# Attention of a two-layer model: values times probabilities in three passes of split operands, two heads side by side

## The reference

```python
q = (hidden_states @ Wq.T).reshape(b, s, NH, HD).transpose(0, 2, 1, 3)
k = (hidden_states @ Wk.T).reshape(b, s, NKV, HD).transpose(0, 2, 1, 3)
v = (hidden_states @ Wv.T).reshape(b, s, NKV, HD).transpose(0, 2, 1, 3)
scores = jnp.einsum('bhqd,bhkd->bhqk', qf, kf)           # k and v repeated for 4 heads each
scores = jnp.where(causal, scores, neg)
attn = jax.nn.softmax(scores, axis=-1).astype(v.dtype)
out = jnp.einsum('bhqk,bhkd->bhqd', attn, v_rep)
out = out.transpose(0, 2, 1, 3).reshape(b, s, NH * HD)
return out @ Wo.T + bo
```

## Time and profile before

| | us |
|---|---|
| median of 3 runs | 1169.13 (1166.28 to 1170.8) |
| the profiled execution | 1162.17 |
| its span, first to last instruction | 1160.4 |
| TensorE busy in the span | 1098.4 (95%) |
| VectorE | 829.4 (71%) |
| ScalarE | 628.2 (54%) |
| GpSimd | 209.6 (18%) |

### The profile page before, as it was taken

The page is one execution under the profiler, slowest core; times in us unless marked ns, Lnnn a source line. Parts: engine busy times, 40 slices in busy tenths (PEclk is TensorE's granted clock), DMA queues, the critical chain, the costliest instruction groups (busy, mean ns, idle before and its releaser), DMA issues. The chain is left out here.

```text
span 1160.4 us, 26495 instructions
## 1 busy us (share of the span) xinstructions
PE 1098.4 (95%) x9990; PEld 937.1 (81%) x9990; DVE 829.4 (71%) x2423; ACT 628.2 (54%) x1607; POOL 209.6 (18%) x246
## 2 busy tenths in 40 slices
PE   6999999999999998999999999959889999998898
PEld 4898899889988998788888889846667777777687
DVE  5777467656765785867776775798998798877454
ACT  5644444444544453544434443457877877766552
POOL 0422222222222221441000000031022102220110
PEclk9999999999999999999999999978899999997899
DMA  9200000000000000201000000011000001100323
GB/s 310 89 6 2 1 1 1 1 1 1 1 1 1 1 1 22 80 1 29 1 1 1 1 1 1 32 60 32 3 34 33 25 10 34 33 2 2 103 69 105
DMA packets 26701, 32.90 MB, mean 28 GB/s; under 512 B 4960, under 2 KB 21968, under 8 KB 26576
## 3 DMA queue, kind: packets, MB, share of 16 engines
q1 hardware_dynamic: 26576, 31.22, 8.6%
HBM read 29.04 MB, written 2.17 MB: 27 GB/s over the span
## 5 line engine op out<-in xcount | busy, mean ns | idle before, releaser
L333 DVE TENSOR_TENSOR a_ps<-a_ps,causal 128x256 f32<-128x256 f32 x128 | 54.6, 427 | 92.8 <-PE a_ps L642 92.8
L1547 PE MATMUL b_ps<-ln_high,b_high 128*128 128x512 f32 x256 | 101.2, 395 | 1.1 <-ACT gate_up_raw L1462 1.1
L692 PE MATMUL a_ps<-a_wo_high,a_oT 128*128 128x256 f32 x512 | 101.2, 282 | 0.1
L1547 PE MATMUL b_ps<-ln_low,b_high 128*128 128x512 f32 x256 | 100.4, 392 | 0.0
L1547 PE MATMUL b_ps<-ln_high,b_low 128*128 128x512 f32 x256 | 100.1, 391 | 0.0
L316 POOL TENSOR_TENSOR a_probs<-a_probs,a_inv 128x256 f32<-128x256 f32 x64 | 40.1, 627 | 330.0 <-DVE a_inv L353 330.0
L1581 PE MATMUL b_ps<-b_wd_high,b_mid 128*128 128x256 f32 x512 | 96.4, 283 | 0.0
L508 ACT CAST a_oT<-a_ps 128x512 fp32r<-128x512 f32 x64 | 37.5, 586 | 107.2 <-PE a_ps L670 107.2
L494 ACT ACTIVATE a_probs<-a_ps,a_negmax 128x128 f32<-128x128 f32 x128 | 47.1, 368 | 89.2 <-DVE a_negmax L339 76.5
L1462 ACT ACTIVATE gate_up_raw<-b_ps 128x512 f32<-128x512 f32 x64 | 37.5, 598 | 95.7 <-PE b_ps L1547 95.6
L1347 DVE TENSOR_TENSOR gate_up_raw<-gate_up_raw,b_ps 128x512 f32<-128x512 f32 x64 | 42.9, 685 | 61.9 <-ACT gate_up_raw L1462 31.9
(11 more groups left out here) (434 smaller groups left out, 3010.0 us busy)
## 6 DMA issues: line engine op xcount, KB each, us to landing
gate_up_raw<-a_scratch SPq DMA_DIRECT2D x8, 768.0 KB, 3.7
gate_up_raw<-in_D_main SPq DMA_DIRECT2D x8, 304.5 KB
x<-in_hidden SPq DMA_DIRECT2D x4, 512.0 KB, 10.7
a_raw<-in_A_q SPq DMA_DIRECT2D x4, 512.0 KB, 7.6
gate_up_raw<-in_A_o SPq DMA_DIRECT2D x1, 2048.0 KB, 13.9
gate_up_raw<-in_B_g SPq DMA_DIRECT2D x1, 2048.0 KB, 12.3
gate_up_raw<-in_B_u SPq DMA_DIRECT2D x1, 2048.0 KB, 8.4
out<-x SPq DMA_DIRECT2D x8, 256.0 KB, 3.1
```

The lines of the kernel that those rows point to most:

```text
L333: nc.vector.tensor_tensor(diagonals, diagonals, r.causal[:].rearrange("p (o k) -> p o k", o=1).to_broadcast([P, 2, P]), ALU.add).then_inc( ...
L692: mm = nc.tensor.matmul(ps[:, out_bank(job), 0:HID], opart, wpart, start=(k == 0 and j == 0), stop=(k == QUARTER - 1 and j == len(passes) ...
L1547: mm = nc.tensor.matmul(ps[:, bank, :], wpart, xpart, start=(j == 0), stop=(j == len(passes) - 1))
```

## The change

- `values` works on a pair of heads and is called in the even steps (for heads `h - 2` and `h - 1`) and behind the last step. `v` and `pT` are kept as high and low parts, and each product becomes three passes with 512 and with 256 columns (two heads side by side).
- ScalarE rounds the turned probabilities (`round_pT`), ahead of the exponentials of the step; in step 15 also those of head 15, ahead of the next keys and queries. VectorE's copy becomes a subtraction. `take_v` on ScalarE gets a subtraction on VectorE behind it (`v_rest_of`), and only that frees the bank.
- The outputs of values of a pair lie in two banks, one for each sequence. `copy_oT` is called in the even steps and `split_oT` in the odd ones, with two instructions of 512 columns each.
- The high parts of `v` and the low part of `pT` live in the place of the gate weights. Of these only expert 2 is loaded where all eight were; the others are issued when the last values are done, and the experts' stage waits for them.

```diff
+FIRST_EXPERT, LATE_EXPERTS = (2, 3), ((3, 8), (0, 2))
...
+        PAIR = 2
+        pT_high = sb("pT_high", [P, GROUP_BATCHES, 3, PAIR, P], F32R)
+        pT_low = at("pT_low", [P, GROUP_BATCHES, 3, PAIR, P], next_weights.raw_at + LATE_EXPERTS[0][0] * EXPERT)
...
-                next_weights.load(sp, 0)
+                next_weights.load(sp, 0, *FIRST_EXPERT)
...
+                sp.wait_ge(next_weights.loaded[0], 16)
+                sp.wait_ge(oT_ready, GROUPS * NH // PAIR)
+                for experts_of in LATE_EXPERTS:
+                    next_weights.load(sp, 0, *experts_of)
...
                 def copy_pT(G):
                     for b in range(GROUP_BATCHES):
-                        dve.wait_ge(pT_ready, 2 * G + b + 1)
-                        if G >= 2:
-                            dve.wait_ge(oT_ready, G - 1)
-                        nc.vector.tensor_copy(pT[:, G % 2, b, :], ps[:, PTB[b], 0:QW]).then_inc(pT_copied, 1)
+                        dve.wait_ge(pT_rounded, 2 * G + b + 1)
+                        if G >= PAIR:
+                            dve.wait_ge(oT_ready, G // PAIR)
+                        nc.vector.tensor_tensor(pT_low[:, b, :, G % PAIR, :], turned_bank(b),
+                                                pT_high[:, b, :, G % PAIR, :].bitcast(F32), ALU.subtract
+                                                ).then_inc(pT_copied, 1)
+
+                def v_rest_of(i, t):
+                    dve.wait_ge(v_rounded, i * GROUP_TILES + t + 1)
+                    nc.vector.tensor_tensor(v_low[t], ps[:, PROJ[t % 2], :], v_high[t].bitcast(F32), ALU.subtract
+                                            ).then_inc(v_taken, 1)
...
-                def split_oT(G):
-
-                    dve.wait_ge(oT_copied, G + 1)
-                    nc.vector.tensor_tensor(oT[:, 1, G % RING, :], ps[:, OTB[G % 2], :],
-                                            oT[:, 0, G % RING, :].bitcast(F32), ALU.subtract).then_inc(oT_split, 1)
+                def split_oT(Q):
+
+                    for b in range(GROUP_BATCHES):
+                        dve.wait_ge(oT_copied, GROUP_BATCHES * Q + b + 1)
+                        nc.vector.tensor_tensor(out_rows(1, Q, b), out_bank_of(b), out_rows(0, Q, b).bitcast(F32),
+                                                ALU.subtract).then_inc(oT_split, 1)
...
-                    if G >= 2:
-                        split_oT(G - 2)
+                    if h % PAIR and G > PAIR:
+                        split_oT(G // PAIR - 1)
+                    if h == 0:
+                        for t in range(GROUP_TILES):
+                            v_rest_of(i, t)
...
+                def round_pT(G):
+                    for b in range(GROUP_BATCHES):
+                        act.wait_ge(pT_ready, 2 * G + b + 1)
+                        if G >= PAIR:
+                            act.wait_ge(oT_ready, G // PAIR)
+                        nc.scalar.copy(pT_high[:, b, :, G % PAIR, :], turned_bank(b)).then_inc(pT_rounded, 1)
...
+                    if h >= 1:
+                        round_pT(G - 1)
                     exps(G, 0)
                     exps(G, 1)
                     if h + 1 < NH:
                         take_q(G + 1)
-                    if G >= 1:
-                        copy_oT(G - 1)
+                    if h % PAIR == 0 and G >= PAIR:
+                        copy_oT(G // PAIR - 1)
...
+                    if h == NH - 1:
+                        round_pT(G)
                     if h == NH - 1 and i < LAST_GROUP:
                         take_k(i + 1, 0)
                         take_q(G + 1)
...
                     for b in range(GROUP_BATCHES):
-                        pe.wait_ge(pT_copied, 2 * G + b + 1)
...
+                        pe.wait_ge(pT_copied, 2 * (G + 1) + b + 1)
+                        turned = [x[:, b].rearrange("p s h q -> p (s h q)") for x in (pT_high, pT_low)]
+                        for t, cols, out in ((2 * b, slice(0, 4 * P), slice(0, 4 * P)),
+                                             (2 * b + 1, slice(4 * P, 6 * P), slice(2 * P, 4 * P))):
+                            passes = split_passes(v_high[t][:, g], v_low[t][:, g], turned[0][:, cols], turned[1][:, cols])
+                            for j, (vpart, ppart) in enumerate(passes):
+                                mm = nc.tensor.matmul(ps[:, OTB[b], out], vpart, ppart, start=(t == 2 * b and j == 0),
+                                                      stop=(t > 2 * b and j == len(passes) - 1))
...
-                    if h >= 1:
-                        values(i, h - 1)
-                    elif i >= 1:
-                        values(i - 1, NH - 1)
+                    if h and h % PAIR == 0:
+                        values(i, h - PAIR)
+                    elif h == 0 and i >= 1:
+                        values(i - 1, NH - PAIR)
...
-                values(LAST_GROUP, NH - 1)
+                values(LAST_GROUP, NH - PAIR)
```

More of the change, by code:

```diff
@@ L208, in attention, with at @@
         qT = later[:, NKV * GROUP:(NKV + 2) * GROUP].rearrange("p (s t) -> p s t", t=GROUP)
-        v_rest = later[:, (NKV + 2) * GROUP:(NKV + 4) * GROUP].rearrange("p (t n) -> p t n", n=NKV * HD)
-        v_first = ahead.xn[:].rearrange("p t d -> p (t d)").rearrange("p (t n) -> p t n", n=NKV * HD)
-        v = [half[:, t, :] for half in (v_first, v_rest) for t in range(GROUP_TILES // 2)]
+        EXPERT = DC * FE * WORD
+        def at(name, shape, offset):
+            return nc.alloc_sbuf_tensor_at("a_" + name, shape, F32R, offset=offset)
+        TWO_TILES = [P, GROUP_TILES // 2, NKV * HD]
+        v_highs = (at("v_high0", TWO_TILES, next_weights.raw_at + LATE_EXPERTS[-1][0] * EXPERT),
+                   at("v_high1", TWO_TILES, next_weights.raw_at + 6 * EXPERT))
+        v_lows = (at("v_low0", TWO_TILES, ahead.xn_at), at("v_low1", TWO_TILES, kept.xnT_at + (NKV + 2) * GROUP * WORD))
+        v_high, v_low = [[half[:, t, :] for half in halves for t in range(GROUP_TILES // 2)] for halves in (v_highs, v_lows)]
         negmax = sb("negmax", [P, 2, GROUP_TILES])
@@ L461, in _ @@
                         add_out(out_jobs(i, h)[1])
-                split_oT(head(LAST_GROUP, NH - 2))
-                split_oT(head(LAST_GROUP, NH - 1))
+                split_oT(GROUPS * NH // PAIR - 1)
                 for job in last_jobs:
@@ L478, in take_v @@
                     if i >= 1:
-                        act.wait_ge(oT_ready, head(i, 0))
-                    nc.scalar.copy(v[t], ps[:, PROJ[t % 2], :]).then_inc(v_taken, 1)
+                        act.wait_ge(oT_ready, head(i, 0) // PAIR)
+                    nc.scalar.copy(v_high[t], ps[:, PROJ[t % 2], :]).then_inc(v_rounded, 1)
+                def round_pT(G):
[4 more added lines that the diff above has]
+                        nc.scalar.copy(pT_high[:, b, :, G % PAIR, :], turned_bank(b)).then_inc(pT_rounded, 1)
                 def take_q(G):
@@ L499, in exps, with copy_oT @@
                                          accum_out=rowsum[:, s, 2 * b + 1:2 * b + 2]).then_inc(exp_ready, 1)
-                def copy_oT(G):
-                    act.wait_ge(oT_ready, G + 1)
-                    if G == 0:
+                def copy_oT(Q):
+                    act.wait_ge(oT_ready, Q + 1)
+                    if Q == 0:
                         act.wait_ge(w_split, len(BLOCKS_AT))
-                    if G >= RING:
-                        act.wait_ge(out_ready, ((G - RING) // QUARTER + 1) * GROUP_TILES)
-                    nc.scalar.copy(oT[:, 0, G % RING, :], ps[:, OTB[G % 2], :]).then_inc(oT_copied, 1)
+                    if PAIR * Q >= RING:
+                        act.wait_ge(out_ready, ((PAIR * Q - RING) // QUARTER + 1) * GROUP_TILES)
+                    for b in range(GROUP_BATCHES):
+                        nc.scalar.copy(out_rows(0, Q, b), out_bank_of(b)).then_inc(oT_copied, 1)
                 def weight_highs(k):
@@ L566, in _ @@
                         take_q(G + 1)
-                copy_oT(head(LAST_GROUP, NH - 1))
+                copy_oT(GROUPS * NH // PAIR - 1)
             @block.tensor
@@ L684, in project_out @@
                         pe.wait_ge(out_taken, job)
-                    pe.wait_ge(oT_split, (quarter + 1) * QUARTER)
+                    pe.wait_ge(oT_split, (quarter + 1) * QUARTER // PAIR * GROUP_BATCHES)
                     rows = slice(t * P, (t + 1) * P)
@@ L1084, in __init__, with load @@
         self.router_loaded = ctx.enter_context(nc.semaphore("router_loaded"))
-    def load(self, sp, k):
-        sp.dma_start(self.raw[:, k], self.sources[k].rearrange("e (c p) f -> p e c f", p=P)
+    def load(self, sp, k, first=0, end=NE):
+        sp.dma_start(self.raw[:, k, first:end], self.sources[k][first:end].rearrange("e (c p) f -> p e c f", p=P)
                      ).then_inc(self.loaded[k], 16)
@@ L1474, in _ @@
                     take_high(k, 0)
+                act.wait_ge(gate_up_weights.loaded[0], 16 * (1 + len(LATE_EXPERTS)))
```

34 lines of the change are left out of this document (21 added, 13 removed).

## The result

The changed kernel takes 1189.81 us (median of 4 runs, 1186.5 to 1199.05), the kernel before 1168.91 beside it (1166.28 to 1170.8): a ratio of 1.020, 95% interval 1.016 to 1.024. Slower by 21 us, as forecast in sign and inside the range of 1173 to 1194; 1183 was forecast, and 1190 lies above the 1178 to 1188 to which the prediction gave its 0.52. Its profiled execution took 1188.63 us (span 1186.7).

A forecast was written before the change was run, and what follows sets the result against it. TensorE, 99% busy, was taken as the bound, with new waits outweighing 17.2 us of saved work: +2.6 for group 0, +4.1 each for groups 1 and 2, group 3 +1.7 and +3.5, together +14: 1183 us, range 1173 to 1194.

The forecast's parts named there:

- The odd step: Steps 5, 7, 9, 11, 13, without values: 4.97 us against 6.07, the next scores released by ScalarE's query copy.
- the even one: Step after an odd one: 6.96 us (+0.89), with a pair's values at 2.08 and transposes 0.12 later for GpSimd.
- keys of steps 1 and 3: Groups 1 to 3: keys wait 1.5 us for VectorE's output job addition, now behind two oT subtractions.
- step 15 stops: At the group's end the next keys come 1.06 us later, TensorE stands 3.3 us; step 15 costs +2.44.
- the output job: In step 15, 2.04 us behind the transposes instead of 0.57, since ScalarE first rounds head 15 and copies keys.
- Rounding and subtracting: Each 384-column piece: 0.49 us for ScalarE's rounding, about 0.55 for VectorE's subtraction, the latter no change from the copy.
- the rival of dearer pieces: Each rounding or subtracting piece takes what 512 columns take (0.58, 0.66), odd steps 0.3 to 0.4 longer: 1190; chance 0.17.
- The clock: TensorE's granted clock stays at 1.00 in the attention, as at the 0.77 us stop; no time counted for a fall.
- its fall at the borders: Rival: 3.3 us stops of step 15 halve the clock, 1.2 us three times, +3.6; 1187 in all, chance 0.15.
- a sign of being wrong: Listed signs: a group of 106, rounding or subtracting beyond 0.6 us, or a clock under 1.00 within the attention.
- The first group's forecast of +2.6: Group 0, no output jobs before step 6: steps 1 and 3 gain 1.27 and 1.36, step 4 loses 1.83; +2.6.
- The last transposes: Group 3's step 15: the last transposes wait 0.49 us more for GpSimd, part of that step's +3.5.

The follow-up runs named there:

- Placement alone: Kernel before, plain fp32 values of two heads together in even steps, their oT copies there and subtractions in odd steps, no rounding or passes: 1185.22 us, ratio 1.0167.
- the two changed orders: Changed kernel, VectorE adding the output job before oT subtractions (steps 1, 3) and earlier in step 15, ScalarE copying keys and queries before rounding head 15: 1168.41 us.
- ScalarE's order alone: Changed kernel, only ScalarE's step 15 altered: next group's keys and queries copied ahead of rounding head 15; 1184.43 us, ratio 1.014 against the kernel before.
- each head by itself: Changed kernel's passes and rounding, but one head's values in every step, passes of 256 and 128 columns: 1178.66 us, ratio 1.009 against the kernel before.
- the values inside the odd steps: Changed kernel, a pair's passes right behind odd steps' scores, ahead of the turning, other engines' orders altered too: 1165.83 us; kernel before in the same order 1172.48.
- the last order: Run with passes inside odd steps, plus layer norm pieces behind the maxima, inversion earlier in steps 10 and 12, layer norm halves swapped: 1161.91 us, ratio 0.9966.

## Why the prediction was right, and which terms were off

**The mechanism held.** The odd step ends on ScalarE's query copy (4.84, forecast 4.97), GpSimd holds the transposes of the even one (7.04, forecast 6.96), values 2.12 (2.08), keys of steps 1 and 3 wait 1.4 us for the addition (1.5), step 15 stops 3.31 us (3.3), the output job starts 1.93 us behind the transposes instead of 0.57 (2.04). Placement alone and the two changed orders show the same from the other side: the waits come with the placement, and put in another order the queues give the 21 us back.

**Where the odd step was off.** 4.97 was forecast for 4.85. The prediction let three of the six transposes end 0.28 us ahead of the last; they are issued 0.109 apart, so it is 0.33, and ScalarE's rounding starts at 1.84, not 1.90. The rest is small change in ScalarE's pitches.

**Rounding and subtracting** at 0.49 and 0.55 were right (0.48 and 0.55 on the mean), so the rival of dearer pieces was wrong, though its 1190 is the nearest to the time measured.

**The clock was the mis-sized term.** The prediction put it at nothing, on the ground that a stop of 0.77 us had left it at 1.00, and gave 0.15 to its fall at the borders (1187). By its own list, a clock under 1.00 within the attention was a sign of being wrong, and that sign came. A stop of 0.77 says little about one of 3.3. The clock fell at all three borders, for 4.4 us where the rival had 3.6, and once where no rival had it, at the last group's wait of 3.62 us. There it cost 2.55: from those transposes to the experts' stage it is 16.35 us (468.60 to 484.95), and 13.80 (468.20 to 482.00) in the run with ScalarE's order alone, where the clock stayed at 1.00. Together 6.9 us. That 14 and 7 make the 21 by which the medians differ is in part luck: by the attention time the change costs 23.2.

The rule of the Trainium skill that the prediction weighed (TensorE: Matmul & The Clock Gate, HAM oscillation: a stream with waits between bursts can fall back to half rate in each round) agrees with the trace at the three borders; with the placement alone one border of three went without it.

**Smaller ones.** Between the two marks the forecast was +14.3 and 23.2 was measured; the clock leaves 2.0 us. Of these 0.9 is step 2 of the first group (7.89, forecast 7.01). In step 1 VectorE splits the output weights beside GpSimd's normalising, whose first piece takes 1.50 us instead of 0.61. It did so in the kernel before too, but after an odd step without values nothing hides it, and the transposes of step 2 wait:

```profile
31.94 1.50 POOL L344 TENSOR_TENSOR a_probs<-a_probs,a_inv 128x256 f32<-128x256 f32 x1 [7.91 <-DVE a_inv L388]
```
```profile
31.78 1.19 DVE L408 TENSOR_TENSOR a_wo_low<-gate_up_raw,a_wo_high 128x1024 fp32r<-128x1024 f32 x1
```
```profile
34.50 0.88 PE L702 MATMUL a_ps<-ident,a_probs 128*128 128x128 f32 x6 [0.74 <-POOL a_probs L346]
```

The rest is 0.1 to 0.2 us in each of steps 0 to 3, against steady pairs 0.05 shorter than forecast. The last transposes stood 7.45 us behind their scores, 6.96 before: the forecast 0.49. The first group's forecast of +2.6 does not follow from the terms that stand beside it, which give +2.2; 4.8 was measured, 1.56 of it the clock.

**What stays open.** Why one stop of 2.81 us left the clock alone and two others did not, why 3.60 us left it alone where 3.40, 3.62 and 3.95 brought it down, and why stops of 1.25 and 0.59 us were enough in the run with each head by itself; and why it stayed low to 238.7 in one run and to 241 in another. From the traces at hand such a term could be given only a chance. The 2 us by which the stages behind the attention were longer in the profiled execution (701.8 against 699.6) lie within what the same stages show in the other kernels (699.6 to 705.3) and are not put down to the change.

## What to carry to other kernels

Before work is taken from the bounding engine or moved on it, ask what hangs over the end of that work on the other engines: here 1.31 us at the end of every step hid three chains, and moving it (18.9 us with nothing else changed) cost more than making it shorter could gain (17.2). In these runs the best place for the block of the bounding engine's work was right ahead of the instruction that waited for the longest chain, and the queues of the others did best to take first what frees a bank. A long stop in a dense stream is to be priced with the products behind it at half rate, as a chance, wherever the trace has no stop of that length.

## What the runs showed of the hardware

Split products of 128 columns came 0.06, 0.11 and 0.11 us apart and held the next by 0.06, so that three of them cost what three of 256 columns (0.1175 each) cost; 512 columns cost 0.23, two heads of 256 side by side no more than their columns.

The layer norm's VectorE operations of four elements take 0.16 us. In each of the four groups the one that starts inside GpSimd's 128x512 normalising takes 0.58 us in the kernel before, 0.94 to 0.96 in the changed one and 0.92 or 0.93 with the values inside the odd steps; its record then ends within 0.02 us of GpSimd's (in the lines above 196.64 + 0.92 = 197.56):

```profile
196.50 1.04 POOL L346 TENSOR_TENSOR a_probs<-a_probs,a_inv 128x512 f32<-128x512 f32 x1
```

Moved to where GpSimd is at rest, in the last order, all four take 0.15 to 0.17.

The granted clock stood at 1.00 (2.4 GHz) or 0.50 (1.2 GHz). After stops of 1.14 us it stayed at 1.00 at every border of two kernels, and after 3.3 us it fell at all six borders of two others; but 1.25 and 0.59 us shortly behind each other brought it down once, and 3.60 us once did not.
